# Means and deviations written to memory element by element, the first rows loaded in halves, and two steps of unit 0 moved

## The chip, the cores and the metric

One core of one Trainium2 chip runs the whole program. The metric is the device time of one execution in microseconds (us). Three runs of the kernel before took 761.16, 761.40 and 761.79 us; the median is 761.4.

## The reference, cut to what matters

`x` is the input `u`, 4 sequences of 1024 tokens with 1024 features, seen as 4096 rows. Each row is normalised (mean subtracted, divided by its deviation), and the normalised rows `xn` go through two branches:

```
xn  = (x - mean) / sqrt(var + 1e-5)                # per row, 1024 features
ug  = xn * sigmoid(xn @ gate_w.T + gate_b)         # attention branch
s   = c * G * cumsum(b * ug / G) + d_eff * ug      # d_eff uses the mean of ug over each sequence
h   = silu(silu(xn @ w1.T) @ w3.T) @ w2.T          # 1024 x 1024 weights
ffn = zeros(4096, 1024); ffn[expert index] += gate share * h   # top 2 of 8 experts, used as row numbers
out = x + s * silu(ffn)
```

Since an expert's index is used as a row number, only the first 8 rows of `ffn` are ever filled; silu(0) = 0, so all other rows of the output equal `x`. The three products of all 4096 rows with 1024 x 1024 weights (w1; the gate, for the first sequence alone; w3) are what takes the time.

## The kernel before, in words

**Tiles and units.** The rows are cut into 4 units of 1024. A pass of products is one unit through one weight matrix. There are 9 passes, numbered n: 0 to 3 are w1 on units 0 to 3, 4 (`GATE`) is the gate on unit 0, and 5 to 8 are w3 on the four units. Each pass is a 2 x 2 block product done with 7 block products instead of 8 (`i` from 0 to 6, in chains that share sums), each of 4 output tiles `j` of 128 x 512. A tile takes 4 times 3 TensorE products of 128x128 with 128x512: every operand is split into a high and a low part (names with r, `wh..`, `wl..`, `x..r`), and the helper `three` (lines 1012 to 1015) multiplies high by high, high by low and low by high.

**Order of the work.** One list, made by `plan()` (lines 90 to 311), holds every step in order; each engine walks through the same list and takes the steps of its kind, with semaphores between engines. So a step's place in the list sets what stands ahead of it on its engine. `at(n, i, j, ...)` hangs a step behind the product tile at place `i`, `j` of pass `n` (`i` counts places in the pass; negative ones reach back into the pass before). The steps before the first tile are written out by hand (lines 250 to 259).

**The start.** Unit 0 is loaded as rows of 128 x 1024 (`ROW`, line 726; rows 0 to 7 each with a buffer or a share of two). VectorE takes the statistics (`NA`, lines 1196 to 1198: two `bn_stats` over halves, one aggregate), or ScalarE does (`NS`, through the helper `squares`, lines 867 to 871), POOL raises the variance to the power -0.5 (lines 822 and 823), VectorE normalises (`NB`, line 1209), TensorE turns the rows (`TR`, line 1033), ScalarE copies the turned rows out of PSUM twice, as high part and as full value (`TE`, lines 881 and 883), and VectorE subtracts for the low part (`TL`, through the helper `tt` at line 1159). The first block of w1 comes in four pieces (`W0`, line 729) and is split by ScalarE (`WH0`, line 887) and VectorE (`WO0`). The first block product of unit 0 is done in halves of 256 tokens (`MP`, two halves of four steps `k`, each step 12 products of 256 columns). `WARM` (line 1023) are turnings of an identity that nobody reads, 34 at the start and 12 before the first `MP`. Later in pass 0 the rows 4 to 7 follow tile by tile, and `LQ` (line 1080) multiplies the router's weights with the turned rows of the unit.

**Units 1 to 3.** They come from memory already turned (`XL`, line 751), so their means and deviations are needed along the free dimension, the same on every partition. For each group of four rows of 128 tokens (rows 8 to 31; half a unit, `h`): the rows are loaded as they are (`ROW`), ScalarE sums and squares them (`STAT`, `squares`), save for rows 11 and 15 (`BN_ROWS`), which VectorE does (lines 1203 to 1205). POOL makes `mvu` of them (`MVC`, lines 834 to 845): 128 partitions x 2 (mean, deviation) x 4 rows. `MV` brings them to memory: TensorE turns `mvu` into PSUM (`spare`, lines 1089 to 1097), ScalarE copies the 8 x 128 result to `mvs` (lines 965 to 970), SP writes it to `mv_d` (line 759). `BC` (line 765) loads it back to all 128 partitions, and VectorE subtracts and multiplies the unit's blocks (`LN`, lines 1233 to 1240). There are six such groups; `MVC` is placed 1 or 2 tiles behind the group's last `STAT`, `MV` and `BC` both 4 or 5 tiles behind it.

**Queues.** SP issues nearly all loads in the list's order, and a wait on SP holds all that stands behind it; ScalarE issues the stores of the tiles (`ST`). ScalarE splits operands (`HI`, `WH`, lines 901 and 914) and VectorE makes their low parts (`LO`, `WO`); the sums of weight blocks are `S`.

Of the kernel before, what the change touches and what calls it, by code (L numbers as in the profile page):

```python
# [5 lines left out]
P = 128  # L6
D = 1024
KT = D // P
TOK = 4096
SEQ = 1024  # L10
UT = 1024
HT = 512
E = 8
# [5 lines left out]

BN_ROWS = (11, 15)  # L20
NU = 4
# [10 lines left out]
ACT = mybir.ActivationFunctionType  # L32
# [57 lines left out]
def plan():  # L90
# [3 lines left out]
    def at(n, i, j, *step):  # L94
        g = 7 * n + i
        extra.setdefault((g // 7, g % 7, j), []).append(step)

    for n in range(NN):
        ln = 0 < n < GATE
        if n == 0:  # L100
# [32 lines left out]
            at(0, 4, 0, "RT", 0)  # L133
            at(0, 4, 0, "WO", 0, 5)
            at(0, 4, 1, "RA", 1)
            at(0, 4, 1, "WH", 0, 6)
            at(0, 4, 1, "HI", 0, 6)
# [3 lines left out]
        else:  # L141
# [9 lines left out]
            if ln:  # L151
# [8 lines left out]
                c = 2 * n  # L160
# [25 lines left out]
        if 0 < n < GATE:  # L186
            if n == 1:
                when = [(0, i, j) for i, j in ((2, 1), (2, 3), (3, 0), (3, 1), (3, 3), (4, 0), (4, 2), (4, 3))]
            else:
                when = [(n - 1, i, j) for i, j in ((-1, 0), (-1, 2), (0, 1), (0, 3), (1, 2), (2, 2), (3, 2), (4, 1))]  # L190
            for t, (m, i, j) in enumerate(when):
                r = n * 8 + t
                at(m, i, j, "STAT", r)
                if r < 8 * GATE - 2:
                    at(m, i, j, "ROW", r + 2)
                if t % 4 == 3:
                    k = 4 * i + j
                    c, v = (1, 4) if r == 11 else (2, 5)
                    at(m, *divmod(k + c, 4), "MVC", 2 * n + t // 4)
                    at(m, *divmod(k + v, 4), "MV", 2 * n + t // 4)  # L200
                    at(m, *divmod(k + v, 4), "BC", 2 * n + t // 4)
# [29 lines left out]
        if n >= GATE:  # L231
            for r in range(8):
                s = 8 * (n - GATE) + r
# [8 lines left out]
    for k in range(3):  # L242
# [44 lines left out]
    for k, (n, i, j) in enumerate(tiles):  # L287
# [4 lines left out]
        p = rank(n, i) % 7  # L292
# [68 lines left out]

def program(nc, x, xT, wB, w11, w2T, small, out):
    steps = plan()
# [9 lines left out]
    def nth(kind, *a):  # L373
        return turn[(kind, *a)]
# [3 lines left out]
    for s in steps:  # L378
        if s[0] == "XL":
            q = place[s[1:]]  # L380
# [23 lines left out]
    mv_d = nc.dram_tensor("mv_d", (2 * NU, 2, HT), F32).ap()  # L404

    with ExitStack() as ctx:
        def sb(name, shape, dt=F32):
            return ctx.enter_context(nc.sbuf_tensor(name, shape, dt))
# [4 lines left out]
        def sem(name):  # L413
            return ctx.enter_context(nc.semaphore(name))
# [40 lines left out]
        y = sb("y", [P, KT, E])  # L455
        mvs = sb("mvs", [E, P])

# [36 lines left out]

        s_row = [sem(f"s_row{i}") for i in range(8)]
        s_pl = [sem(f"s_pl{i}") for i in range(PLACES)]
        s_wl = [sem(f"s_wl{i}") for i in range(7)]
# [46 lines left out]
        s_mv = sem("s_mv")  # L544
        s_mvt = sem("s_mvt")
        s_mvs = sem("s_mvs")
        s_mvd = sem("s_mvd")
# [25 lines left out]
        def row_buf(r):  # L573
            if r in (4, 5) or r >= 8:
                return rows[:, r % 2, :]
            p = (6, 6, 5, 5, None, None, 4, 4)[r]
            return w_f(p, 0)[:, 2 * (r % 2):2 * (r % 2) + 2, :].rearrange("p a n -> p (a n)")

        def row_loaded(wait, r):
            if r < 8:  # L580
                wait(s_row[r], 16)
            else:
                wait(s_row[4 + r % 2], 16 * ((r - 8) // 2 + 2))
# [131 lines left out]
        def _(eng):  # L715
            wait = Waiter(eng)
            ncopy = 0
            for s in steps:
                kind = s[0]
                if kind == "ROW":  # L720
# [3 lines left out]
                    elif r >= 8:  # L724
                        wait(s_tr, 2 * (r - 3))
                    eng.dma_start(row_buf(r), x[r * P:(r + 1) * P, :]).then_inc(s_row[r if r < 8 else 4 + r % 2], 16)
                elif kind == "W0":
# [29 lines left out]
                elif kind == "MV":  # L757
                    wait(s_mvs, nth(*s))
                    eng.dma_start(mv_d[s[1]].rearrange("r (t p) -> (r t) p", p=P), mvs[:, :]).then_inc(s_mvd, 16)
                elif kind == "BC":  # L760
# [35 lines left out]
        def _(eng):  # L796
# [20 lines left out]
            for s in steps:  # L817
# [13 lines left out]
                elif kind == "MVC":  # L831
# [4 lines left out]
                    if k > 2:  # L836
                        wait(s_mvt, k - 2)
                    if last in BN_ROWS:
# [19 lines left out]
        def _(eng):  # L858
# [3 lines left out]
            def link(ins):  # L862
                count[0] += 1
                ins.then_inc(s_ac, 1)
                wait(s_ac, count[0])

            def squares(row, total, square, where):
# [5 lines left out]
            for s in steps:  # L873
# [79 lines left out]
                elif kind == "STAT":  # L953
# [10 lines left out]
                    squares(row_buf(r), acs[:, h, 0, t:t + 1], acs[:, h, 1, t:t + 1], row_buf(r)).then_inc(s_st2, 1)  # L964
                elif kind == "MV":
                    k = nth(*s)
                    wait(s_mvt, k)
                    if k > 1:
                        wait(s_mvd, 16 * (k - 1))
                    eng.activation(mvs[:, :], spare[0:E, 0:P], ACT.Copy).then_inc(s_mvs, 1)  # L970
                elif kind == "LE":
# [37 lines left out]
        def _(eng):  # L1009
# [7 lines left out]
            for s in steps:  # L1017
                kind = s[0]
                if kind == "WARM":
                    wait(s_id, 1)  # L1020
                    idle = main[0] if s[1] else spare
                    for q in range(12 if s[1] else 34):
                        eng.transpose(idle[:, q % 4 * P:(q % 4 + 1) * P], ident[:, :], ident[:, :])
# [59 lines left out]
                elif kind == "RA":  # L1083
# [4 lines left out]
                    ins.then_inc(s_ra, 1)  # L1088
                elif kind == "MV":
                    k = nth(*s)  # L1090
                    wait(s_mv, k)
                    if k > 1:
                        wait(s_mvs, k - 1)
                    else:
                        wait(s_ter, 16)
                    eng.matmul(spare[0:E, 0:P], mvu[:, (k - 1) % 2, :, :].rearrange("p r t -> p (r t)"), ident[:, :],
                               start=True, stop=True).then_inc(s_mvt, 1)
                elif kind == "PH":
# [3 lines left out]
                    wait(s_rt, 2 * NU)  # L1102
                    wait(s_mvs, 2 * (NU - 1))
                    u = n - L2
# [43 lines left out]
        def _(eng):  # L1148
# [3 lines left out]
            def link(ins):  # L1152

                count[0] += 1
                ins.then_inc(s_dv, 1)
                wait(s_dv, count[0])
# [32 lines left out]
            for s in steps:  # L1189
                kind = s[0]  # L1190
                if kind == "NA":
                    t = s[1]
                    row_loaded(wait, t)
                    src = row_buf(t)
                    st = bst[:, nth(*s) % 2, :]
                    eng.bn_stats(st[:, 0:6], src[:, 0:HT])
                    link(eng.bn_stats(st[:, 6:12], src[:, HT:D]))
                    eng.bn_aggr(mv0[:, t, :], st).then_inc(s_na, 1)
# [293 lines left out]
```

## Time and profile before

| | |
|---|---|
| median of 3 runs | 761.4 us |
| profiled execution | 761.42 us |
| its span (first to last instruction) | 759.6 us |
| instructions | 8804 |
| granted TensorE clock, mean | 1.000 |
| products with 128x512 or 128x256 columns (lines 1013 to 1015) | 3 x 1024 |

Times in the profile are counted from the start of the span. PE is TensorE's products, PEld its weight loads, DVE is VectorE, ACT ScalarE, POOL GpSimd, SPq the queue of SyncE. A row of the timeline gives its start, its length, engine, line, operation, result and operands (buffer numbers as the allocator gave them), how many like it follow without a break, and in brackets the idle time of the engine just before it and what ended that. Products overlap: what counts for TensorE's pace is the distance from one start to the next, not the length of a row. The rows' names are those of buffers: `wh6f` and `wh5f` hold the first rows of x, `wl2f` the first block of w1, `x0f` to `x8f` the blocks of a unit, `x3r` and `x5r` the low parts at the start.

### The profile page before, as it was taken

To read this page: it belongs to the slowest core of one execution; us is meant where nothing else is said; L and a number is where in the kernel's file an instruction comes from. 1 tells how busy PE (TensorE), PEld (TensorE's weight loads), DVE (VectorE), ACT (ScalarE), POOL (GpSimd) and SP (SyncE) were. 2 spreads that over 40 slices of the span, in tenths; PEclk is the share of its full clock that TensorE was granted. 3 is DMA by queue.
4 is the path that set the end of the run, shared out by engine and by line. 5 is a ranking of instruction groups with operands and counts; after the bars stand their busy time and mean duration, and the time that the engine had idled before them with its cause. 6 is when DMAs were issued, how large, how long until landed. Compare 5 with 4: busy or idle time off the path is not lost.

```text
span 759.6 us, 8804 instructions
## 1 busy us (share of the span) xinstructions
PE 749.9 (99%) x3580; PEld 597.8 (79%) x3580; DVE 508.2 (67%) x477; ACT 343.2 (45%) x441; POOL 41.8 (6%) x56
## 2 busy tenths in 40 slices
PE   8999999999999999999999999999999999999997
PEld 7867877887788787888788878878788778877875
DVE  6889888775958485469999997574525462456321
ACT  5869674845572425232943372225123331324122
POOL 3302103020301000000000000000000000000000
PEclk9999999999999999999999999999999999999999
DMA  9644763547442534466596713241231323110500
GB/s 353 266 167 167 265 228 131 205 143 225 150 156 94 194 112 152 192 209 234 197 360 207 287 56 138 111 153 42 110 139 48 146 84 121 45 56 1 223 1 3
DMA packets 27400, 117.20 MB, mean 154 GB/s; under 512 B 3440, under 2 KB 3680, under 8 KB 20320
## 3 DMA queue, kind: packets, MB, share of 16 engines
q1 hardware_dynamic: 18112, 99.85, 36.5%
q10 hardware_dynamic: 9248, 16.80, 5.9%
q8 instruction: 28, 0.46, 0.3%
q14 instruction: 12, 0.10, 0.0%
HBM read 95.60 MB, written 37.77 MB: 176 GB/s over the span
## 4 chain that ended last, share of the span: by engine, by line
PE 82%; DVE 10%; issue 4%; ACT 3%; DMA 0%; POOL 0%; DVEq 0%
PE main L1013 26%; PE main L1015 26%; PE main L1014 26%; PE lgp L1080 1%; PE spare L1107 1%; PE lgp L1107 1%; DVE x3r L1159 1%; DVE x2f L1159 1%; DVE wl3f L1159 1%; DVE x1f L1159 1%; DVE wl5f L1159 1%; DVE x8f L1159 0%; PE main L1142 0%; DMA wh6f<-x 0%; DVE s L1159 0%
## 5 line engine op out<-in xcount | busy, mean ns | idle before, releaser
L1159 DVE TENSOR_TENSOR s<-s,main 128x512 f32<-128x512 f32 x72 | 48.5, 683 | 60.1 <-PE main L1015 60.1
L1159 DVE TENSOR_TENSOR u<-u,main 128x512 f32<-128x512 f32 x36 | 24.4, 685 | 41.8 <-PE main L1015 41.8
L922 ACT ACTIVATE s<-main 128x512 f32<-128x512 f32 x36 | 20.8, 596 | 55.1 <-PE main L1015 23.4
L941 ACT ACTIVATE u<-u 128x512 f32<-128x512 f32 x32 | 20.2, 632 | 54.5 <-DVE u L1159 54.4
L1159 DVE TENSOR_TENSOR u<-s,main 128x512 f32<-128x512 f32 x32 | 21.7, 685 | 32.5 <-PE main L1015 32.5
L941 ACT ACTIVATE rows<-rows 128x512 f32<-128x512 f32 x16 | 10.1, 632 | 71.3 <-DVE rows L1159 71.3
L941 ACT ACTIVATE s<-s 128x512 f32<-128x512 f32 x32 | 20.0, 630 | 47.8 <-DVE s L1159 47.8
L1159 DVE TENSOR_TENSOR rows<-s,main 128x512 f32<-128x512 f32 x16 | 11.0, 688 | 30.4 <-PE main L1015 30.4
L941 ACT ACTIVATE u<-main 128x512 f32<-128x512 f32 x32 | 18.7, 592 | 20.5 <-PE main L1015 20.5
L871 ACT ACTIVATE rows<-rows,nm 128x1024 f32<-128x1024 f32 x22 | 25.4, 1154 | 0.7
L869 ACT ACTIVATE rows<-rows 128x1024 f32<-128x1024 f32 x23 | 24.2, 1050 | 0.1
L1013 PE MATMUL main<-x2r,wh0r 128*128 128x256 f32 (+1 forms) x48 | 15.7, 326 | 1.1 <-DVE x3r L1159 0.8
L855 POOL MEMSET tail<- 128x1024 f32 x1 | 1.0, 955 | 269.9 <-PE main L1015 269.9
L1015 PE MATMUL main<-x2r,wl0r 128*128 128x256 f32 (+1 forms) x48 | 15.2, 318 | 0.0
L1159 DVE TENSOR_TENSOR x6r<-x6f,x4r 128x2048 fp32r<-128x2048 f32 x3 | 6.9, 2289 | 8.8 <-ACT x4r L901 8.8
L1013 PE MATMUL main<-x6r,wh3r 128*128 128x512 f32 x32 | 12.5, 392 | 0.0
L1014 PE MATMUL main<-x6r,wh0r 128*128 128x512 f32 x32 | 12.5, 390 | 0.0
L1015 PE MATMUL main<-x6r,wl3r 128*128 128x512 f32 x32 | 12.5, 389 | 0.0
L1014 PE MATMUL main<-x5r,wh1r 128*128 128x512 f32 x32 | 12.5, 389 | 0.0
L1014 PE MATMUL main<-x5r,wh2r 128*128 128x512 f32 x32 | 12.5, 389 | 0.0
L1014 PE MATMUL main<-x4r,wh4r 128*128 128x512 f32 x32 | 12.4, 389 | 0.0
L1014 PE MATMUL main<-x8r,wh3r 128*128 128x512 f32 x32 | 12.4, 389 | 0.0
(703 smaller groups left out, 2427.1 us busy)
## 6 DMA issues: line engine op xcount, KB each, us to landing
out<-x SPq DMA_DIRECT2D x31, 512.0 KB, 7.9
rows<-x SPq DMA_DIRECT2D x26, 512.0 KB, 4.3
H_d<-u ACTq DMA_DIRECT2D x32, 256.0 KB, 3.9
H_d<-s ACTq DMA_DIRECT2D x16, 256.0 KB, 3.7
rows<-xh_d SPq DMA_DIRECT2D x16, 256.0 KB, 5.2
w2f<-w2T SPq DMA_DIRECT2D x2, 2048.0 KB, 9.8
wl6f<-wB SPq DMA_DIRECT2D x3, 1024.0 KB, 8.2
wl4f<-wB SPq DMA_DIRECT2D x3, 1024.0 KB, 6.0
```

The lines of the kernel that those rows point to most:

```text
L855: eng.memset(tb[:, 0:D], 0.0).then_inc(s_oz, 1)
L869: link(eng.activation(row, row, ACT.Copy, accum_out=total))
L871: return eng.activation(where, row, ACT.Square, bias=nm[:, 0:1], accum_out=square)
L922: eng.activation(s1[:, j, :], bk, ACT.Copy).then_inc(s_pa, 1)
L941: ins = eng.activation(dst, src, ACT.Silu)
L1013: eng.matmul(o, sh, mh, start=first, stop=False, skip_group_check=True)
L1014: eng.matmul(o, sh, ml, start=False, stop=False, skip_group_check=True)
L1015: return eng.matmul(o, sl_, mh, start=False, stop=last, skip_group_check=True)
L1080: ins = eng.matmul(lgp[h][Q * q:Q * (q + 1), :], wr32[:, NQ * kh + q, :], xf(n, b)[:, q, :], start=(kh == 0), stop=(kh == 1))
L1107: ins = eng.matmul(acc[o][Q * j:Q * (j + 1), :], Pz[:, 8 * u + 4 * h + j, :], c_buf(n, i, j), start=(u == 0 and h == 0), stop=(u == NU - 1 ...
L1159: return eng.tensor_tensor(o, a, b, op)
```

## The change

- **Means to memory.** `MV` becomes one transfer of SP alone, straight from `mvu` to `mv_d`: 128 partitions x 2 x 4 single elements of 4 bytes. TensorE's turning, ScalarE's copy, `mvs` and their semaphores go. `MV` waits for POOL's `MVC`, and is placed `c + 2` tiles behind the last `STAT`, one tile earlier than before and one ahead of `BC`. POOL waits for the transfer before it writes a buffer of `mvu` again.
- **Rows 0 and 1 in halves.** Each is loaded by two transfers of 128 x 512 from a new input `x01` that holds these halves one after the other; the first `bn_stats` waits for the first half alone.
- **Order at the start.** `NA` of row 2 goes behind the low parts of rows 0 and 1, `WO0` of step 1 ahead of them; `WO0` of step 2 and `NA` of row 3 follow. `WARM` has 29 and 14 turnings for 34 and 12.
- **A Silu first.** ScalarE does one Silu on a column before its other steps; its result is written over later.
- **Unit 0's pieces.** Row 15's statistics go from VectorE to ScalarE and two places later (from place 4, tile 3 to place 5, tile 1), with the load of row 17; `WH` of block 6 goes one tile earlier (from place 4, tile 1 to tile 0).

```diff
-BN_ROWS = (11, 15)
+BN_ROWS = (11,)
...
+            at(0, 4, 0, "WH", 0, 6)
             at(0, 4, 1, "RA", 1)
-            at(0, 4, 1, "WH", 0, 6)
...
-                when = [(0, i, j) for i, j in ((2, 1), (2, 3), (3, 0), (3, 1), (3, 3), (4, 0), (4, 2), (4, 3))]
+                when = [(0, i, j) for i, j in ((2, 1), (2, 3), (3, 0), (3, 1), (3, 3), (4, 0), (4, 2), (5, 1))]
...
-                    c, v = (1, 4) if r == 11 else (2, 5)
+                    c, v = (1, 4) if r in (11, 15) else (2, 5)
                     at(m, *divmod(k + c, 4), "MVC", 2 * n + t // 4)
-                    at(m, *divmod(k + v, 4), "MV", 2 * n + t // 4)
+                    at(m, *divmod(k + c + 2, 4), "MV", 2 * n + t // 4)
                     at(m, *divmod(k + v, 4), "BC", 2 * n + t // 4)
...
-             ("WH0", 0), ("WH0", 1), ("TE", 0, 0), ("TE", 1, 0), ("WO0", 0), ("NA", 2), ("TL", 0, 0), ("TL", 1, 0), ("MP", 0, 0),
-             ("WH0", 2), ("WO0", 1), ("MP", 0, 1), ("WH0", 3), ("TE", 0, 1), ("TE", 1, 1), ("NA", 3), ("NB", 2),
-             ("WO0", 2), ("MP", 0, 2), ("NB", 3), ("TR", 2), ("TR", 3), ("WO0", 3), ("MP", 0, 3), ("WH", 0, 1),
+             ("WH0", 0), ("WH0", 1), ("TE", 0, 0), ("WO0", 0), ("TE", 1, 0), ("WO0", 1), ("TL", 0, 0), ("TL", 1, 0), ("MP", 0, 0), ("MP", 0, 1),
+             ("NA", 2), ("WH0", 2), ("WO0", 2), ("MP", 0, 2), ("NA", 3), ("WH0", 3), ("TE", 0, 1), ("TE", 1, 1),
+             ("NB", 2), ("TR", 2), ("WO0", 3), ("NB", 3), ("TR", 3), ("MP", 0, 3), ("WH", 0, 1),
...
+                    c0 = 0
+                    if r < 2:
+                        c0 = HT
+                        eng.dma_start(row_buf(r)[:, 0:HT], x01[r, 0]).then_inc(s_rh[r], 16)
+                    src = x01[r, 1] if r < 2 else x[r * P:(r + 1) * P, :]
+                    eng.dma_start(row_buf(r)[:, c0:D], src).then_inc(s_row[r if r < 8 else 4 + r % 2], 16)
...
                 elif kind == "MV":
-                    wait(s_mvs, nth(*s))
-                    eng.dma_start(mv_d[s[1]].rearrange("r (t p) -> (r t) p", p=P), mvs[:, :]).then_inc(s_mvd, 16)
+                    k = nth(*s)
+                    wait(s_mv, k)
+                    if k > 1:
+                        wait(s_mvd, 16 * (k - 1))
+                    eng.dma_start(mv_d[s[1]].rearrange("r (t p) -> p r t", p=P), mvu[:, s[1] % 2, :, :],
+                                  allow_slow_non_contiguous=True).then_inc(s_mvd, 16)
...
+            wait(s_po, 3)
+            eng.activation(nm[:, :], mhalf[:, 0:1], ACT.Silu)
...
-                elif kind == "MV":
-                    k = nth(*s)
-                    wait(s_mvt, k)
-                    if k > 1:
-                        wait(s_mvd, 16 * (k - 1))
-                    eng.activation(mvs[:, :], spare[0:E, 0:P], ACT.Copy).then_inc(s_mvs, 1)
...
-                    for q in range(12 if s[1] else 34):
+                    for q in range(14 if s[1] else 29):
...
-                    eng.matmul(spare[0:E, 0:P], mvu[:, (k - 1) % 2, :, :].rearrange("p r t -> p (r t)"), ident[:, :],
-                               start=True, stop=True).then_inc(s_mvt, 1)
...
+                    if t < 2:
+                        wait(s_rh[t], 16)
+                    else:
+                        row_loaded(wait, t)
                     eng.bn_stats(st[:, 0:6], src[:, 0:HT])
+                    row_loaded(wait, t)
                     link(eng.bn_stats(st[:, 6:12], src[:, HT:D]))
```

## Rows read from the trace of the kernel before

**Rows 1.** The page, first lines: span, then busy time (share) and instructions of each engine.

```profile
span 759.6 us, 8804 instructions
...
PE 749.9 (99%) x3580; PEld 597.8 (79%) x3580; DVE 508.2 (67%) x477; ACT 343.2 (45%) x441; POOL 41.8 (6%) x56
```

**Rows 2.** Waits of PE: line, what it waited for, us in total, times, longest.

```profile
PE main L1013 <- DVE x3r L1159: 1.1, 2, 0.8
...
PE main L1013 <- DVE x6r L1159: 0.4, 1, 0.4
```

**Rows 3.** Timeline of the first 21 us, several engines.

```profile
4.10 0.69 DVE L1196 BATCH_NORM_STATS2 bst<-wh6f 128x6 f32<-128x512 f32 x1 [4.10 <-DMA wh6f<-x]
...
6.99 1.27 ACT L887 ACTIVATE wh0r<-wl2f 128x512 fp32r<-128x512 f32 x2 [4.97 <-DMA wl2f<-w]
...
9.91 0.69 DVE L1196 BATCH_NORM_STATS2 bst<-wh5f 128x6 f32<-128x512 f32 x1
...
10.64 0.59 ACT L883 ACTIVATE x0f<-lgp 128x512 f32<-128x512 f32 x1
...
11.35 1.24 DVE L1159 TENSOR_TENSOR x3r<-x0f,x2r 128x512 fp32r<-128x512 f32 x2
...
12.65 0.39 PE L1013 MATMUL main<-x2r,wh0r 128*128 128x256 f32 x1 [0.79 <-DVE x3r L1159]
...
16.38 0.81 DVE L1209 TENSOR_SCALAR wh5f<-wh5f,mv 128x1024 f32<-128x1024 f32 x1 [0.46 <-POOL mv L823]
...
17.50 0.60 PE L1033 MATMUL main<-ident,wh5f 128*128 128x128 f32 x4
...
20.98 0.39 PE L1013 MATMUL main<-x2r,wh0r 128*128 128x256 f32 x1
```

**Rows 4.** Timeline around 40 us, ScalarE and PE.

```profile
36.95 1.28 ACT L941 ACT_TABLE_LOAD   x1
...
42.82 1.06 PE L1080 MATMUL lgp<-x0f,cst 128*32 128x512 f32 x8 [1.26 <-ACT x7f L883]
```

**Rows 5.** PE's timeline around one turning, then the group of all of them.

```profile
171.75 0.39 PE L1014 MATMUL main<-x2r,wh5r 128*128 128x512 f32 x1
171.97 0.39 PE L1015 MATMUL main<-x0r,wl5r 128*128 128x512 f32 x1
172.29 0.38 PE L1096 MATMUL spare<-ident,mvu 128*8 128x128 f32 x2
...
172.94 0.39 PE L1014 MATMUL main<-x2r,wh5r 128*128 128x512 f32 x1
...
L1096 PE MATMUL spare<-ident,mvu x12: 272/274/276, 75.1 to 254.8; 128*8 128x128 f32 x12
```

**Rows 6.** Waits of SP's queue: us in total, times, longest.

```profile
SPq L759 <- ACT mvs L970: 25.5, 6, 9.4
```

**Rows 7.** Timeline of SP's queue, 75 to 86 us.

```profile
76.14 0.43 SPq L751 DMA_DIRECT2D x4f<-xT  x1
...
84.14 0.35 SPq L759 DMA_DIRECT2D mv_d<-mvs  x1
...
85.37 0.34 SPq L765 DMA_DIRECT2D bc<-mv_d  x1
```

**Rows 8.** Landings: of the broadcast (KB, median us); of the w2 loads (shortest, median, longest).

```profile
bc<-mv_d SPq DMA_DIRECT2D x6, 512.0 KB, 3.8
...
DMA to landing us min/median/max: 7.5/9.8/12.1
```

**Rows 9.** Timeline of VectorE, 82 to 92 us.

```profile
82.19 2.29 DVE L1159 TENSOR_TENSOR wl6r<-wl6f,wh6r 128x2048 fp32r<-128x2048 f32 x1 [1.91 <-ACT wh6r L914]
...
87.20 0.69 DVE L1203 BATCH_NORM_STATS2 bst<-rows 128x6 f32<-128x512 f32 x1
...
91.19 4.61 DVE L1159 TENSOR_TENSOR x2f<-x2f,bc 128x2048 f32<-128x2048 f32 x2
```

**Rows 10.** The chain of waits: start, us, what; one 256-column product.

```profile
16.47 0.12 PE main L1015
```

More of the change, by code:

```diff
@@ L359, in places_of, with program @@
     raise ValueError("no place for the last rows")
-def program(nc, x, xT, wB, w11, w2T, small, out):
+def program(nc, x, x01, xT, wB, w11, w2T, small, out):
     steps = plan()
@@ L455, in program @@
         y = sb("y", [P, KT, E])
-        mvs = sb("mvs", [E, P])
         def w_f(p, part):
@@ L495, in program @@
         s_row = [sem(f"s_row{i}") for i in range(8)]
+        s_rh = [sem(f"s_rh{i}") for i in range(2)]
         s_pl = [sem(f"s_pl{i}") for i in range(PLACES)]
@@ L544, in program @@
         s_mv = sem("s_mv")
-        s_mvt = sem("s_mvt")
-        s_mvs = sem("s_mvs")
         s_mvd = sem("s_mvd")
@@ L725, in _ @@
                         wait(s_tr, 2 * (r - 3))
-                    eng.dma_start(row_buf(r), x[r * P:(r + 1) * P, :]).then_inc(s_row[r if r < 8 else 4 + r % 2], 16)
+                    c0 = 0
[4 more added lines that the diff above has]
+                    eng.dma_start(row_buf(r)[:, c0:D], src).then_inc(s_row[r if r < 8 else 4 + r % 2], 16)
                 elif kind == "W0":
@@ L836, in _ @@
                     if k > 2:
-                        wait(s_mvt, k - 2)
+                        wait(s_mvd, 16 * (k - 2))
                     if last in BN_ROWS:
@@ L1088, in _ @@
                     ins.then_inc(s_ra, 1)
[L1089 to L1095, printed above, removed]
-                    eng.matmul(spare[0:E, 0:P], mvu[:, (k - 1) % 2, :, :].rearrange("p r t -> p (r t)"), ident[:, :],
-                               start=True, stop=True).then_inc(s_mvt, 1)
                 elif kind == "PH":
@@ L1102, in _ @@
                     wait(s_rt, 2 * NU)
-                    wait(s_mvs, 2 * (NU - 1))
                     u = n - L2
@@ L1192, in _ @@
                     t = s[1]
-                    row_loaded(wait, t)
                     src = row_buf(t)
                     st = bst[:, nth(*s) % 2, :]
+                    if t < 2:
+                        wait(s_rh[t], 16)
+                    else:
+                        row_loaded(wait, t)
                     eng.bn_stats(st[:, 0:6], src[:, 0:HT])
+                    row_loaded(wait, t)
                     link(eng.bn_stats(st[:, 6:12], src[:, HT:D]))
@@ L1480 @@
         "x": np.ascontiguousarray(t["L0_attn_u"].reshape(TOK, D)),
+        "x01": np.ascontiguousarray(t["L0_attn_u"].reshape(TOK, D)[:2 * P].reshape(2, P, 2, HT).transpose(0, 2, 1, 3)),
         "xT": np.ascontiguousarray(t["L0_attn_u"].reshape(NU, 2, HT, 2, 4, P).transpose(0, 3, 1, 5, 4, 2)),
```

## The prediction

> **What bounds the kernel now.** I read the page first: TensorE is busy for 99% of the span, VectorE for 67%, ScalarE for 45% [rows 1]. A busy PE is a modelled figure here, so I went on to the waits of PE and to the timelines, to find where its instructions start later than the ones before them allow. Away from a few places one 128x512 product starts 0.22 to 0.23 us after the other, all the way to the end. The time is therefore the sum of what PE has to do, plus its start, plus those few places, and an edit pays only if it takes work or a hole from PE. The reader should see four of them.
>
> First, the start. PE begins the first product at 12.65 and the fifth step of products at 20.98, both times held by VectorE's x3r [rows 2, 3]. Second, a hole of 1.26 us before the logits at 42.82, ended by a ScalarE copy (x7f); ScalarE loaded a table for 1.28 us just ahead of that copy, at 36.95 [rows 4]. Third, 0.4 us at the first product of unit 1, again ended by VectorE (x6r) [rows 2]. Fourth, the turning itself: from 171.97 to 172.94 two products and the turning start, 0.97 us where two starts at 0.22 to 0.23 would be 0.45. So one turning costs PE 0.52 us, far more than its two passes, because the products on either side of it are spaced wider too; twelve records are two for each of six [rows 5].
>
> The profiled execution took 761.42 us, its span 759.6; the median of the three runs shown is 761.4, so a sum made against the profile needs no correction.
>
> **The change, part by part.**
>
> *The turning goes.* Six times 0.52 us leave PE, 3.1 us in all, and PE has no other work to wait for there. ScalarE loses the six copies behind them, SP's wait for those copies (25.5 us in six times [rows 6]) becomes a wait for POOL, which is done before ScalarE's copy. What comes in is a transfer of 2x4 single elements from each of 128 partitions, 1024 pieces, where eight pieces of 512 bytes went. No row shows a transfer of single elements. Below: the present one lands at most 1.23 us after its issue, since the broadcast that waits for it is issued at 85.37 against 84.14 [rows 7]. Above: the two w2 loads, 512 pieces of 4 KB each, landed after 7.5 and 12.1 us [rows 8]; they are the same number of pieces with a thousand times the bytes. A gain on today's 1.23 is excluded, since nothing in it is taken away. I take 3 us, nearer the lower row, because the pieces carry four bytes.
>
> What does that cost? Nothing as long as the broadcast is in time. The tightest case is the first one. SP stands at that point right behind the x4f load, issued at 76.14 [rows 7], which will be about 74 with the 2.1 us that the start and the table load bring (below). The broadcast lands 3.8 us after its issue [rows 8], with 0.3 for issuing. Its user is the subtraction at 91.19 [rows 9]. VectorE will come to it 2.1 us earlier for the same reason, up to 1.9 for a wait that goes and 1.4 for statistics that go, so at 85.8; but the adds ahead of it wait for PE's tiles, which come 2.1 + 0.5 earlier, so 88.6 at the latest. I take 87. That leaves 87 - 74 - 4.1, some 9 us for the transfer, three times what I take. If it needs more, LN is late first, then the products of unit 1. Behind SP's wait stand row loads and the next x blocks; as long as the transfer stays under those 9 us SP is freed earlier than today.
>
> The Trainium skill (DMA: Bandwidth & Descriptors, Rules for kernel authors) speaks against this edit: a strided last dimension makes one descriptor per element, and one should arrange it otherwise; for a transposition by rearranged access it names a 19-fold difference. That would be an estimate of 19 x 1.23, some 23 us, and the sum would lose all its gain; no run so far shows it.
>
> *The start.* Rows 0 and 1 come as two halves. The first statistics begin when all of row 0 has landed, at 4.10 [rows 3]. With halves the first one (0.69 us) can lie beside the second half's transfer. It gains between nothing, or a little less with two more issues on SP, and 0.69; I take 0.5, since its second half may still have to be awaited a little. That carries to the turned rows. Next, the statistics of row 2 stand at 9.91 and hold VectorE for 1.44 us, until the two x3r at 11.35 [rows 3]. Moved behind them, x3r waits instead for ScalarE's copy that starts at 10.64 and takes 0.59, so 11.23, with the 0.5 about 10.7. The second x3r then ends about 11.4 and PE starts at 11.5 in place of 12.65. The warm-up turnings (29 for 34, 14 for 12) only fill PE's waits on either side.
>
> Not all of that lasts. VectorE now does row 2's and row 3's statistics later, and row 3's normalisation, at 16.38 behind POOL [rows 3], comes at about 16.7. But PE could turn rows 2 and 3 only at 17.50, behind the third step of products, though row 3 was ready at 17.19. Now the third step is done at 11.5 + 36 x 0.12 = 15.8 (one 256-column product takes 0.12 in the chain [rows 10]), row 2 is turned at once and row 3 at 17.5 to 17.6, where it had stood behind row 2's eight turnings, at some 18.4 by estimate. From there the old distance to 20.98 gives 20.1: 0.9 us gained. The ends are 0.3 (the halves bring nothing and VectorE's row 3 keeps its 0.3 us of delay) and 1.4 (PE never waits again from 11.4 on: 48 products of 0.12 and sixteen turnings at 0.60 for four [rows 3] end at 19.6).
>
> *The table load.* A Silu on ScalarE ahead of all else puts its table there at the start, where ScalarE waits 4.97 us for weights anyway [rows 3]. The 1.28 us at 36.95 go. The copies of the last two rows come that much earlier, and the hole at 42.82 closes but for some 0.1: 1.2 us from PE. That only holds if copies and squares do not call the old table back; after 36.95 they run with Silu and no third load appears in the trace. The Trainium skill (ScalarE: Activation LUTs, What ACT_TABLE_LOAD costs) gives a switch some 2.66 us with its drain; the trace has 1.28 and the next instruction right behind it, so I take 1.28, and the hole is the limit either way.
>
> *Two pieces of unit 0.* Row 15's statistics go from VectorE (1.44 us as at 9.91, here from 87.20) to ScalarE, which is busy for less than half of the span and has room there; the split of wh6 is issued one tile earlier, so VectorE's 1.91 us wait at 82.19 goes [rows 9]. VectorE then reaches unit 1's blocks before PE does, and the 0.4 us at its first product [rows 2] go. If that cover fails, the 0.4 us stay and up to another 0.5 joins them.
>
> **The sum.** 0.9 + 1.2 + 0.4 + 3.1 = 5.6 us, and 761.42 - 5.6 = 755.8.
>
> **The rivals.**
>
> *Halves bring nothing.* The transfers may follow one another no faster, and the two extra issues push the weights back. For it: ScalarE waits at 6.99 for the first weights [rows 3], so DMA sets the pace there too. Against it: the statistics order alone shortens the wait for x3r. Then the start gives 0.3 or nothing, and the time is 756.4 to 756.7.
>
> *The single elements come late (slower than before).* This is one mechanism: if an engine's 64 elements are not streamed but each waits for its write, at a quarter of 1.23 us apiece, a transfer takes 64 x 0.31 + 1.2 = 21 us. The first broadcast is then 12 us beyond its 9, PE waits for unit 1, and the time is 755.8 + 12, about 768. It decides from 9 us on, and from 9 + 5.6 + 1.5 = 16 us (0.23 us an element) the kernel is slower than before. For it speaks that no row shows such pieces; against it, that 512 pieces landed in 7.5 us with 4 KB each. The skill's warning named above is this rival, with its own figure of 23 us and some 770.
>
> *The table load stays.* If the compiler loads a table for the copies again, the 1.2 us stay: 757.0. The single load in the trace behind the first Silu speaks against it.
>
> **How the numbers follow.** Forecast as summed: 0.64, with its own range 754.6 to 757. Halves bring nothing: 0.15. Late elements: 0.14, of which 0.03 stay below 759.9, 0.03 come out within 0.2% of now and 0.08 above. Table load stays: 0.05. The rest, 0.02, is something that I don't see, most likely near no change. Below, the start at its far end (1.4) and the whole 1.3 us hole give 755.2, and waits too small for the view may close with them, so 754.4; above, a forecast without start and table load gives 757.9, and a transfer of 12 us, 3 beyond its 9, gives 758.8. So 754.4 to 759.2. A measurement of this kernel tells 0.2%, or 1.5 us, from no change: faster by more 0.64 + 0.15 + 0.05 + 0.03 = 0.87, within it 0.03 + 0.02 = 0.05, slower 0.08.
>
> **What would show it.** Right: no PE record of the turning, products at 0.23 us through those places; first product near 11.5, the fifth step near 20.1; one table load, at the start; the logits of unit 0 near 40.7 with a wait of a tenth; broadcast issued within 5 us of the element transfer. Wrong: SP waiting over 9 us at the broadcast, VectorE's first subtraction in unit 1 released by a DMA, a second table load near 35, or the first statistics still at 4 us.

## The result, and the profile after

The change takes 766.4 us, median of 6 runs (765.3 to 767.9), beside 761.4 for the kernel before on the same chip: 1.0068 of its time, 95% interval 1.0058 to 1.0079. It is slower by 5 us, where 755.8, a gain, was forecast, and it lies outside the range of 754.4 to 759.2. The profiled execution took 766.27 us.

The first lines of the page of the changed kernel, to be held against [rows 1]:

```profile
span 764.2 us, 8759 instructions
...
PE 749.1 (98%) x3565; PEld 598.1 (78%) x3565; DVE 507.0 (66%) x474; ACT 342.1 (45%) x440; POOL 39.8 (5%) x54
```

TensorE's busy time fell by less than 1 us, while the span grew by 4.6: it stands still more than before. Two steps of the chain of waits of the changed kernel, from 74 to 101 us (start, us, what), say where:

```profile
74.93 14.67 DMA mv_d<-mvu
...
89.62 6.45 DMA bc<-mv_d
```

VectorE's timeline behind it:

```profile
96.17 4.62 DVE L1154 TENSOR_TENSOR x2f<-x2f,bc 128x2048 f32<-128x2048 f32 x2 [8.34 <-DMA bc<-mv_d]
```

The first transfer of single elements, issued behind the load of x4f (1024 KB), lands after 14.67 us. The broadcast that waits for it needs 6.45 more, and VectorE's subtraction starts at 96.17 instead of 91.19 [rows 9], after 8.34 us without work. That a DMA releases it is a sign that the prediction named for being wrong; so is a wait of SP of over 9 us at the broadcast, at most 11.1 here. The queue of SP and the landings of the transfer (line 765) in the changed kernel show how the row load beside it fared:

```profile
74.46 0.43 SPq L754 DMA_DIRECT2D x4f<-xT  x1
74.93 0.43 SPq L765 DMA_DIRECT2D mv_d<-mvu  x1
78.44 0.34 SPq L729 DMA_DIRECT2D rows<-x  x1
89.62 0.33 SPq L772 DMA_DIRECT2D bc<-mv_d  x1
...
DMA to landing us min/median/max: 10.6/11.7/14.7
```

All six transfers are slow, 10.6 us at best. The row load issued at 78.44 landed 12.9 us later, where the same load took 4.5 before; ScalarE stood 5.67 us for it. Broadcasts land after 6.3 us in the median, 3.8 before [rows 8]. All DMA of the core is slow in that stretch. From 80 to 89.5 us, in the changed kernel and then in the kernel before (the last two columns are the busy share of the DMA engines and the GB/s that they moved):

```profile
80.00:89.50 9.50, 9.50 (x44) 7.86 (x43) 6.28 (x8) 5.44 (x10) 0.00 (x0) 1.00 0.77 34
```

```profile
80.00:89.50 9.50, 9.50 (x43) 7.86 (x43) 7.56 (x10) 7.83 (x12) 0.52 (x3) 1.00 0.63 219
```

The engines count as busy, but they move 34 GB/s instead of 219.

What it costs TensorE stands in its waits and its timeline around 100 us:

```profile
PE main L1018 <- DVE u L1154: 4.1, 2, 3.5
```

```profile
97.59 0.39 PE L1020 MATMUL main<-x5r,wl6r 128*128 128x512 f32 x1
101.44 0.79 PE L1018 MATMUL main<-x5r,wh6r 128*128 128x512 f32 x1 [3.46 <-DVE u L1154]
102.03 0.63 PE L1019 MATMUL main<-x7r,wh6r 128*128 128x512 f32 x1
102.46 0.63 PE L1020 MATMUL main<-x5r,wl6r 128*128 128x512 f32 x1
...
106.30 0.63 PE L1020 MATMUL main<-x5r,wl6r 128*128 128x512 f32 x1
108.76 0.50 PE L1018 MATMUL main<-x1r,wh0r 128*128 128x512 f32 x1 [1.84 <-DVE x6r L1154]
```

The wait at 101.44 is not for the late data. It is for the add `u`, with which VectorE takes a finished tile out of PSUM and which stands behind the late subtraction in VectorE's order. After the wait the products start 0.43 us apart instead of 0.23. The stretch before the wait and the one behind it have the granted clock in the column after POOL's busy time:

```profile
92.00:97.60 5.60, 5.60 (x27) 4.62 (x25) 1.43 (x1) 2.98 (x7) 1.47 (x3) 1.00 1.06 363
101.40:106.50 5.10, 5.06 (x12) 3.80 (x12) 5.07 (x4) 4.92 (x7) 0.00 (x0) 0.50 0.53 60
```

The granted clock was 0.50, that is 1.2 GHz, for the twelve products from 101.44 on. At 108.76 TensorE waits again, for x6r, which VectorE makes after the subtractions.

**The account.** What TensorE's starts lost from 97 us on, beyond its pace before: 3.6 at 101.44; 2.6 in the slow products (0.36 + 11 x 0.20); 2.2 at 108.76; 0.84 at 166.59 and 0.69 at 221.08: 9.9 us. Against it stand 1.7 that start and table load gave (the first product with `wh4` comes at 67.30, before at 68.99), 3.1 for the turnings and 0.5 for the old hole in unit 1: 9.9 - 5.3 = 4.6, the growth of the span.

The other edits did what they say. The Silu's table load stands at the start of ScalarE, and the logits of unit 0 begin without a wait (compare [rows 4]); two rows of the changed kernel's timeline:

```profile
0.74 1.28 ACT L876 ACT_TABLE_LOAD   x1 [0.74 <-PEq L1466]
...
41.17 1.06 PE L1085 MATMUL lgp<-x0f,cst 128*32 128x512 f32 x8
```

The start gained less than forecast. Its timeline in the changed kernel, to be read against [rows 3]:

```profile
3.64 0.70 DVE L1194 BATCH_NORM_STATS2 bst<-wh6f 128x6 f32<-128x512 f32 x1 [3.64 <-DMA wh6f<-x]
...
6.38 0.69 DVE L1196 BATCH_NORM_STATS2 bst<-wh6f 128x6 f32<-128x512 f32 x1 [0.32 <-DMA wh6f<-x]
...
12.20 0.38 PE L1018 MATMUL main<-x2r,wh0r 128*128 128x256 f32 x1
...
17.32 0.81 DVE L1208 TENSOR_SCALAR wh5f<-wh5f,mv 128x1024 f32<-128x1024 f32 x1 [0.46 <-POOL mv L830]
...
18.19 0.66 PE L1038 MATMUL lgp<-ident,wh5f 128*128 128x128 f32 x4 [0.55 <-DVE wh5f L1208]
...
20.75 0.39 PE L1018 MATMUL main<-x2r,wh0r 128*128 128x256 f32 x1
```

The first half of row 0 is there 0.46 us earlier, but the second half of row 1 has to be awaited until 6.38. The first product comes 0.45 us earlier; row 3 is normalised 0.94 later than before, and at the fifth step 0.23 us are left.

### The profile page after: what moved, and what is told of

Same layout as the page of the kernel before. It is cut to its first block, busy times and chain, and to the rows that moved or that the text cites. A ratio compares the mean times of both kernels' runs of the same rounds, so it can differ in the third digit from the quotient of the medians.

```text
span 764.2 us, 8759 instructions
## 1 busy us (share of the span) xinstructions
PE 749.1 (98%) x3565; PEld 598.1 (78%) x3565; DVE 507.0 (66%) x474; ACT 342.1 (45%) x440; POOL 39.8 (5%) x54
## 4 chain that ended last, share of the span: by engine, by line
PE 74%; DVE 10%; DMA 7%; issue 4%; ACT 4%; POOL 0%; SPq 0%; ACTq 0%; DVEq 0%
PE main L1018 23%; PE main L1020 23%; PE main L1019 23%; DMA mv_d<-mvu 2%; DMA bc<-mv_d 2%; DMA H_d<-x6f 2%; DMA x7f<-xT 1%; DVE x1f L1154 1%; PE spare L1102 1%; PE lgp L1102 1%; PE lgp L1085 1%; DVE x8f L1154 1%; DVE x6f L1154 1%; DVE x5r L1154 1%; DVE x2f L1154 1%
## 5 line engine op out<-in xcount | busy, mean ns | idle before, releaser
L850 POOL TENSOR_SCALAR mvu<-acs 128x4 f32<-128x4 f32 (+1 forms) x6 | 7.3, 1216 | 158.0 <-ACT rows L882 157.9
L952 ACT ACTIVATE x6f<-x6f 128x512 f32<-128x512 f32 x8 | 4.9, 624 | 17.0 <-DVE x6f L1154 17.0
```

The lines of the kernel that those rows point to most:

```text
L850: eng.tensor_scalar(mvu[:, h, 0, 0:m], acs[:, h, 0, 0:m], 1.0 / D, None, ALU.mult)
L952: ins = eng.activation(dst, src, ACT.Silu)
```

## The experiments

Times are medians beside the kernel before on the same chip. It took 761.3 to 761.5 us in every batch, so runs of different batches are compared as they are.

**1. The change without its new transfer.** TensorE's turning, ScalarE's copy and the transfer of eight pieces are kept, all else is as in the change.

```diff
-                    eng.dma_start(mv_d[s[1]].rearrange("r (t p) -> p r t", p=P), mvu[:, s[1] % 2, :, :],
-                                  allow_slow_non_contiguous=True).then_inc(s_mvd, 16)
+                    eng.dma_start(mv_d[s[1]].rearrange("r (t p) -> (r t) p", p=P), mvs[:, :]).then_inc(s_mvd, 16)
```

> The change with TensorE's turning kept for the means (TensorE, ScalarE copy, eight runs of 512 bytes); all else as in the change. Theory (the single elements land too slowly, all else of the change is good): no late broadcast, no long wait of PE, so before less the table load (1.3), the start (0.2 as seen) and unit 0's hole (0.4): 759.3 us, between 758.8 and 760.0. Rival (the moved pieces of unit 0, row 15 on ScalarE above all, make VectorE or PE wait): the wait of PE near 97 us stays and the time is 762 or more.

759.83 us, 0.9982 of before (0.9972 to 0.9991). TensorE begins unit 1 without a wait, at a granted clock of 1.00 from 90 to 110 us; in this kernel:

```profile
101.69 0.50 PE L1023 MATMUL main<-x1r,wh0r 128*128 128x512 f32 x1
```

So the loss is the transfer's, and the other edits together gain 1.5 us (761.33 before in this batch).

**2. The new transfer alone**, in the kernel before (the reverse edit).

> The kernel before with the transfer of single elements alone. Theory: the transfer lands 10 us or more after its issue, VectorE waits some 8 us for the first broadcast and PE for some 4 to 6 us in unit 0's last block, less 3.1 us of turnings: 763 to 769 us. Rival (the order is at fault, not the transfer): the turnings leave, nothing else happens, 758.3 us.

765.82 us, 1.0056 (1.0041 to 1.0071). The same landings and much the same loss without any of the other edits, but what is late first is another transfer: VectorE, which here still takes row 15's statistics, stands 4.06 us for that row and then only 0.84 us for the broadcast. The landings of line 759, and VectorE's wait, in this kernel:

```profile
DMA to landing us min/median/max: 10.3/11.6/14.7
```

```profile
91.13 0.69 DVE L1188 BATCH_NORM_STATS2 bst<-rows 128x6 f32<-128x512 f32 x1 [4.06 <-DMA rows<-x]
```

**3. 256 pieces of 16 bytes.** Four neighbouring tokens go to each partition (the rows are loaded in another order), so a partition's four values are one run in memory.

```diff
                     src = x01[r, 1] if r < 2 else x[r * P:(r + 1) * P, :]
+                    if r >= 8:
+                        g = r // 4
+                        src = x[4 * g * P:4 * (g + 1) * P, :].rearrange("(p t) n -> t p n", t=4)[r % 4]
-                    eng.dma_start(mv_d[s[1]].rearrange("r (t p) -> p r t", p=P), mvu[:, s[1] % 2, :, :],
+                    eng.dma_start(mv_d[s[1]].rearrange("r (p t) -> p r t", t=4), mvu[:, s[1] % 2, :, :],
```

> The change, but each statistics load takes rows 4p+t to partition p, so that a partition's four means lie side by side and go as runs of 16 bytes: 256 pieces instead of 1024; nothing else is moved. Theory (landing time goes with the number of pieces, about 10 us for 1024): it lands in 3.5 to 4.5 us, no broadcast is late, 756.0 to 757.0 us. Rival (the order or SP's place is at fault): PE's long wait stays, over 762 us. Rival (the landing goes with the partitions or with writing to memory at all): it lands in 8 to 12 us as now, over 760 us.

758.55 us (757.47 to 760.77), 0.9967 (0.9958 to 0.9977): a gain, but 1.5 us above the upper end expected. The profiled execution is the slowest of the ten, so its waits may be longer than those of the others. The landings of line 768, and the waits of VectorE and TensorE, in this kernel:

```profile
DMA to landing us min/median/max: 3.5/5.0/8.0
```

```profile
90.89 4.62 DVE L1157 TENSOR_TENSOR x2f<-x2f,bc 128x2048 f32<-128x2048 f32 x2 [2.48 <-DMA bc<-mv_d]
...
103.49 0.50 PE L1021 MATMUL main<-x1r,wh0r 128*128 128x512 f32 x1 [2.20 <-DVE x6r L1157]
```

The slowest is again the first, 8.0 us. It was issued at 77.29, half a microsecond behind the load of x4f on the same queue; its broadcast left at 85.27 and took 5.5 us, so VectorE stood for it.

**4. 512 pieces of 8 bytes.** Only the write differs from the change: two neighbouring values of a partition go side by side. The row loads are not reordered with it, so the means reach other tokens than their own; the kernel serves for its time alone.

> The change with the same bytes moved as 512 pieces of 8 bytes; the means and deviations arrive in another order of tokens. Theory (landing goes with the number of pieces): 6 to 7 us from issue to landing, under the 9 us that I had found free, so hardly a wait of PE: 756 to 758 us. Rival (not the pieces): 11 to 12 us as now and 764 us or more.

759.69 us in its one run, 1.7 above what was expected, with landings of 3.9, 5.9 and 9.3 us (shortest, median, longest). Twice the pieces of run 3 land less than 1 us later in the median (5.9 against 5.0), and twice these again, in the change, 6 later. So the landing doesn't go with the number of pieces; what single elements have beside their number was left to runs 11 and 12. A wait of TensorE of 2.66 us, by the starts, was left at the head of unit 1.

**5. Pieces of 16 bytes, the first transfer one step earlier**, ahead of the load of x4f, and its broadcast one step earlier.

```diff
+                    early = r == 11
-                    at(m, *divmod(k + c + 2, 4), "MV", 2 * n + t // 4)
-                    at(m, *divmod(k + v, 4), "BC", 2 * n + t // 4)
+                    at(m, *divmod(k + c + 2 - early, 4), "MV", 2 * n + t // 4)
+                    at(m, *divmod(k + v - early, 4), "BC", 2 * n + t // 4)
```

> The element-free form with 16-byte pieces (256 of them), and for the first group only the transfer is issued one step earlier, ahead of the load of x4f, and the broadcast one step earlier too. Theory (the landing is the queue ahead plus the pieces): the first transfer is issued at about 73.5 us instead of 77.3, lands in 3.5 to 4.5 us instead of 8.0, bc is in SBUF by 85, VectorE's wait of 2.48 us for bc at 90.9 and TensorE's of 2.36 us at 101 to 103.5 go, and the seven products at half clock behind it run at full clock: 754.8 to 755.8 us. Rival (a transfer of many pieces delays what is queued with it, whenever it is issued, so the load of x4f or the broadcast is late instead): TensorE still stands still for over 1.5 us between 90 and 104 us, 757.5 to 758.8 us.

756.39 us, 0.9938 (0.9924 to 0.9953); the kernel is 0.6 us above the upper end expected, but all the waits named are gone. SP's queue, the first landing (line 769), and VectorE's subtraction in this kernel:

```profile
73.15 0.38 SPq L769 DMA_DIRECT2D mv_d<-mvu  x1
...
76.09 0.43 SPq L758 DMA_DIRECT2D x4f<-xT  x1
76.56 0.43 SPq L776 DMA_DIRECT2D bc<-mv_d  x1
...
DMA to landing us min/median/max: 2.2/2.2/2.2
```

```profile
87.98 4.61 DVE L1158 TENSOR_TENSOR x2f<-x2f,bc 128x2048 f32<-128x2048 f32 x2
```

Ahead of the megabyte the same transfer lands in 2.2 us instead of 8.0. VectorE comes to the subtraction at 87.98 and waits for nothing; the prediction had it there at 87.

**6. Single elements, the first transfer one step earlier**: the edit of run 5 in the change itself.

> The change as it is, with 1024 single elements, but the first group's transfer and broadcast one step earlier, the transfer ahead of the load of x4f. Theory (the pieces themselves take the time): the first transfer, issued at about 73 us, still needs 10 us or more, the broadcast is issued at 83 to 84.5 us and lands by 88 to 91, so the waits of 3.5 us of TensorE and the half clock behind them mostly go: 757 to 760 us; transfers queued while the pieces drain are late. Rival (the queue ahead made most of the 14.7 us): it lands in 6 to 7 us, no wait is left, 755.5 to 756.5 us. Second rival (early or late, the pieces hold other transfers up so that row 15 becomes the late one): 763 us or more.

767.65 us, 1.0082 (1.0067 to 1.0097): worse than the change, the last of the three ways expected. Rows of SP's queue, then of VectorE and ScalarE, in this kernel:

```profile
73.95 0.39 SPq L766 DMA_DIRECT2D mv_d<-mvu  x1
...
84.96 0.33 SPq L773 DMA_DIRECT2D bc<-mv_d  x1
```

```profile
92.64 4.62 DVE L1155 TENSOR_TENSOR x2f<-x2f,bc 128x2048 f32<-128x2048 f32 x2 [3.80 <-DMA bc<-mv_d]
...
86.80 1.06 ACT L881 ACTIVATE rows<-rows 128x1024 f32<-128x1024 f32 x1 [4.51 <-DMA rows<-x]
```

With nothing of a megabyte ahead of it the transfer still holds the broadcast back for 11.0 us, so these are the pieces' own; the queue ahead made the other 4 of the 14.7. Now the load of x4f is behind the elements, and loads of x4f land after 11.3 us in the median (6.4 in run 5). The rows are late for ScalarE too. An earlier place did not mend a transfer that holds up its neighbours.

**7. Rows 0 and 1 whole**, and the start in the order of before, in the kernel of run 1.

> The change with TensorE's turning kept (the kernel of the first run) and, in addition, rows 0 and 1 loaded whole, in the order of the start of the kernel before. If the halves bring what the traces show at the fifth step (20.79 us with them, 20.79 to 20.98 without), this runs at 759.8 to 760.2 us, within 0.3 us of the kernel with halves (759.83). If they bring the 0.9 us of the prediction, 760.6 to 760.9 us.

759.44 us, 0.9974 (0.9965 to 0.9984), which the intervals can't tell from run 1's 759.83. The fifth step begins at 21.02 here, 20.79 there. The halves and the new order of the start bring nothing that the time shows.

**8. Without the first Silu**, in the kernel of run 1.

```diff
-            wait(s_po, 3)
-            eng.activation(nm[:, :], mhalf[:, 0:1], ACT.Silu)
```

> The change with TensorE's turning kept and without the early Silu on ScalarE. If the table load stood on the path as predicted, it is back at about 37 us, the wait of TensorE at about 42 us of 1.2 us is back, and the time is 760.9 to 761.2 us (1.2 more than 759.83). Rival (the first load at the start is only moved, and a later wait takes up the gain): within 0.3 us of 759.83.

760.89 us, 0.9993 (0.9983 to 1.0003): 1.06 more than run 1. The table load is back at 37.09, and so is the wait, in TensorE's timeline of this kernel:

```profile
42.95 1.07 PE L1088 MATMUL lgp<-x0f,cst 128*32 128x512 f32 x8 [1.33 <-ACT x7f L891]
```

**9. Row 15's sums and W(0,6) in their old places**, in the kernel of run 1.

> The change with TensorE's turning kept, and with the two pieces of unit 0's work back in their old places (row 15's sums on VectorE, the rounding of W(0,6) one step later). If they are worth what the prediction gave them, the wait of 0.4 us of TensorE in unit 1 is back: 760.1 to 760.4 us against 759.83. Rival (the wait was hidden by what comes behind it): within 0.2 us of 759.83.

760.23 us, 0.9986 (0.9976 to 0.9996): 0.4 more than run 1, no more than the 0.39 by which run 7 was faster, so the times alone can't tell them apart. What tells them apart is the wait in TensorE's timeline, 0.36 us here and none in run 1 at the same product:

```profile
102.32 0.50 PE L1023 MATMUL main<-x1r,wh0r 128*128 128x512 f32 x1 [0.36 <-DVE x6r L1169]
```

**10. Run 5 with rows 0 and 1 whole** and the start of before.

> 16-byte pieces, the first transfer one step earlier, rows 0 and 1 whole in the old order of the start; the table load and the two pieces of unit 0 as in the change. If the halves cost a little, as the last comparison has it (759.44 without against 759.83 with), 755.9 to 756.2 us. Rival (the halves bring the 0.23 us that the first trace showed): 756.5 to 756.8 us.

756.18 us, 0.9931 (0.9916 to 0.9946; 756.11 to 756.26): 5.25 us faster than before, the fastest here, and again no worse without the halves. The gap to run 7, which differs in the way of the means to memory alone (with the order of the row loads and the earlier first broadcast that go with it), is 3.26 us. Product by product, TensorE's lead over run 7 grows in steps of 0.41 to 0.49 us at the six turnings, 2.6 in all; smaller steps between them make the rest.

**11. The transfer by itself.** Seven extra transfers that nothing reads, one after the other, in the kernel of run 10, between 660 and 700 us:

```diff
+                    eng.dma_start(pr_d[2, 0:1024].rearrange("(q p t) -> p q t", p=P, t=2), one.rearrange("p (q t) -> p q t", t=2),
+                                  allow_slow_non_contiguous=True).then_inc(s_pr, 16)
+                    wait(s_pr, 48)
+                    eng.dma_start(pr_d[3, 0:512].rearrange("(q p) -> p q", p=P), one[:, 0:4],
+                                  allow_slow_non_contiguous=True).then_inc(s_pr, 16)
+                    wait(s_pr, 64)
...
```

> The kernel of the run before with seven extra transfers from mvu to memory that nothing reads, in the stretch from 660 to 700 us in which no other transfer of SyncE is queued, each issued when the one before has landed: 256 pieces of 16 bytes twice, 512 of 8, 512 of 4, 1024 of 4, 1024 of 8, 256 of 4. Theory A (the size of 4 bytes is what is slow): 512 of 4 bytes take 5 us or more, 1024 of 8 bytes under 7 us, 1024 of 4 bytes 10 to 11 us. Theory B (the number of pieces in one transfer is what is slow, past 512): 512 of 4 bytes land in about 4 us as 512 of 8 do, and 1024 of 8 bytes take 10 to 11 us as 1024 of 4 do. Under either 256 pieces land in 2 to 3.5 us. The kernel's own time stays that of the run before unless the seven together pass 698 us.

SP's queue in this kernel; each issue waits for the landing before, so the distance to the next row is the landing (16 bytes twice, then 512 x 8, 512 x 4, 1024 x 4, 1024 x 8, 256 x 4 bytes):

```profile
660.43 0.43 SPq L792 DMA_DIRECT2D pr_d<-mvu  x1
665.22 0.37 SPq L795 DMA_DIRECT2D pr_d<-mvu  x1
666.86 0.36 SPq L798 DMA_DIRECT2D pr_d<-mvu  x1
670.60 0.36 SPq L801 DMA_DIRECT2D pr_d<-mvu  x1
680.17 0.36 SPq L804 DMA_DIRECT2D pr_d<-mvu  x1
690.23 0.36 SPq L807 DMA_DIRECT2D pr_d<-mvu  x1
694.42 0.36 SPq L810 DMA_DIRECT2D pr_d<-mvu  x1
```

The first transfer stood behind a load of x8f, issued at 660.07, and took 4.8 us; the same 256 pieces of 16 bytes with nothing ahead took 1.6, 512 of 8 bytes 3.7, 1024 of 8 bytes 4.2. But 512 of 4 bytes took 9.6, 1024 of 4 bytes 10.0, and 256 of 4 bytes still 7.8. It is not the number; by this run it is the 4 bytes. The kernel itself took 756.16 us in its one run.

The time does not go into sending the pieces. For the 512 of 4 bytes, issued at 670.60, two stretches of this kernel (the last two columns are the busy share of the DMA engines and GB/s):

```profile
671.40:671.90 0.50, 0.50 (x4) 0.38 (x4) 0.00 (x0) 0.38 (x1) 0.00 (x0) 1.00 0.50 4
671.90:680.10 8.20, 8.20 (x38) 6.80 (x37) 3.76 (x2) 3.60 (x4) 0.00 (x0) 1.00 0.00 0
```

All their packets lie in the first half microsecond; then the engines carry nothing for 8.2 us until the landing is reported.

**12. 4 bytes, side by side or 64 bytes apart**, in the same place.

```diff
+                    eng.dma_start(pr_d[1, 0:512].rearrange("(q p) -> p q", p=P), one[:, 0:4],
+                                  allow_slow_non_contiguous=True).then_inc(s_pr, 16)
+                    eng.dma_start(pr_d[2, :].rearrange("(q p u) -> p q u", p=P, u=16)[:, :, 0:1],
+                                  one[:, 0:4].rearrange("p (q t) -> p q t", t=1), allow_slow_non_contiguous=True).then_inc(s_pr, 16)
```

> The kernel of the probe with other extra transfers in the same stretch, each issued when the one before has landed: 256 pieces of 16 bytes (behind the load of x8f), 512 of 4 bytes to adjacent addresses, 512 of 4 bytes to addresses 64 bytes apart, 512 of 8 bytes 64 bytes apart, 128 of 4 bytes adjacent, 256 of 16 bytes. Theory (the size of a piece alone decides): 512 of 4 bytes take 9 to 10 us at either spacing, and 128 of 4 bytes over 5 us. Rival (4-byte pieces are slow where neighbouring pieces, sent by different partitions, go into the same 64 bytes): 512 of 4 bytes 64 bytes apart take 3 to 5 us like 512 of 8 bytes. 256 of 16 bytes take 1.6 us again.

SP's queue in this kernel, in the order of the expectation, from the second on:

```profile
664.98 0.37 SPq L794 DMA_DIRECT2D pr_d<-mvu  x1
673.08 0.36 SPq L797 DMA_DIRECT2D pr_d<-mvu  x1
676.39 0.36 SPq L800 DMA_DIRECT2D pr_d<-mvu  x1
678.43 0.33 SPq L803 DMA_DIRECT2D pr_d<-mvu  x1
685.25 0.36 SPq L806 DMA_DIRECT2D pr_d<-mvu  x1
```

The theory that the size alone decides falls. 512 single elements to adjacent addresses took 8.1 us, the same 512 set 64 bytes apart 3.3; 512 of 8 bytes 64 bytes apart took 2.0, and only 128 adjacent single elements still 6.8. What is slow is a single element of 4 bytes written next to others; 8 bytes to adjacent addresses were not (3.7 in run 11). In every slow case the neighbour came from another partition; whether that matters was not varied. Each number is one landing, and repeated forms differ by up to 1.6 us (16 bytes with nothing ahead: 1.6 and 3.2; 512 adjacent single elements: 9.6 and 8.1), which doesn't touch 3.3 against 8.1. Why such neighbours are slow, and whether spacings between 4 and 64 bytes are, stays open.

## Why the prediction was wrong

**The step that failed** is the landing of the single elements: "I take 3 us, nearer the lower row, because the pieces carry four bytes." It is 11.7 in the median and 14.7 where it matters. Two things were missed. The size counted the wrong way: pieces of 16 bytes land in 1.6 us and pieces of 8 in 3.7, adjacent single elements in 7.8 to 10.0 (run 11). And the lower row, 1.23 us, was read from a transfer that went out with nothing fresh ahead of it; the new one stands right behind the load of x4f, which the prediction itself noted, and that adds some 4 to 6 us (14.7 against 11.0 in run 6, 8.0 against 2.2 in runs 3 and 5). The upper row was no bound either: its loads are 512 pieces each, half of the new transfer's 1024, and 14.7 lies above their 12.1.

**The limit of 9 us** was derived well on VectorE's side: it is at the subtraction at 87.98 in run 5, forecast 87. But it took the broadcast's 3.8 us as given. In runs 3 and 4 the broadcast took 5.5 and 6.3 us, and landings of 8.0 and 9.3 already made VectorE stand for 2.48 and 2.77.

**The rival "single elements come late"** named what was late, with its break-even at 16 us. Its mechanism, each element waiting for its write in turn, does not fit: 256, 512 and 1024 elements took 7.8, 9.6 and 10.0 us, and the packets are sent within half a microsecond (run 11). By its line 14.7 us, 5.7 beyond the 9, would give 761.5; the change took 766.4. Three costs came on top that the line didn't hold: the broadcast itself landed in 6.45 instead of 3.8 us, TensorE ran twelve products at half clock after its wait (2.6 us), and there were two later stops. The one of 0.84 stands behind a late load of x7f, which SP could issue only after its wait for the third transfer; the one of 0.69 is for a copy of ScalarE, and what it has to do with the landings is not shown.

**The Trainium skill** (DMA: Bandwidth & Descriptors, Rules for kernel authors) spoke against the edit, and by that it was the better guide: one descriptor per element was slow here, by 10.6 against at most 1.23 us, a factor of 8.6 at least where the estimate had 19. Its remedy, a contiguous last dimension, is what run 3 does with four values, and with run 5's place 256 pieces of 16 bytes gave the whole gain. But its reason is not the whole of it here: 512 single elements set 64 bytes apart, single packets as well, landed in 3.3 us (run 12).

**The turnings**: forecast 3.1 us; runs 7 and 10 differ by 3.26. Right, and 2.6 of it stand as steps at the six turnings. The price was read from the spacing of starts, not from the turning's own rows.

**The table load**: forecast 1.2; run 8 shows 1.06 and the 1.33 us wait back. Right, and no second load was called for.

**The two pieces of unit 0**: forecast 0.4; in run 9 the wait of 0.36 is back. Right by the trace; the 0.40 between the times is within what they vary by.

**The start**: forecast 0.9; the trace shows 0.23 at the fifth step, and the time none (runs 7 and 10 against 1 and 5). The rival "halves bring nothing" was right on this part. Here the step that failed is "with the 0.5 about 10.7": row 1's second half had to be awaited until 6.38, so the two x3r are done 0.7 us later than forecast, and the first product came at 12.20 instead of 11.5. Then row 2's statistics, moved behind the low parts, came at 12.06 instead of 9.91, and row 3's normalisation at 17.32 instead of the 16.7 forecast, so TensorE waits for row 3 at 18.19.

With the transfer mended, the sum without the start's 0.9 would be 4.7 us, 756.7; run 10 took 756.18. So the other three terms of the sum held.

## What to carry to other kernels

Give each partition a run of neighbouring values before writing statistics to memory: here pieces of 16 bytes landed in 1.6 to 3.2 us with nothing ahead (2.8 to 6.5 among the other loads of run 10), adjacent single elements in 6.8 to 10.0 (10.6 to 14.7 in the change), and the order of the rows could be chosen at load time at no cost that the time shows. Bound a small transfer's landing together with the large one issued just ahead of it on its queue, and put the small one first; that helped the pieces of 16 bytes (run 5) and not the single elements (run 6). When a wait is to be priced, add what the waiting engine has queued behind it, what other transfers lose meanwhile, and products at half clock, which followed some of TensorE's waits here.

## What was not expected of the hardware

- Single elements of 4 bytes were slow side by side, not for their size alone: 8.1 us for 512 of them adjacent, 3.3 with 64 bytes between their starts.
- Until such a transfer has landed, others land late too, on both queues: a row load took 12.9 us, 4.5 before, and ScalarE's stores of x6f took 11.4 us in the median, 3.8 before. The pieces themselves were sent long since.
- The granted clock fell to 0.50 (1.2 GHz) after TensorE's wait of 3.6 us, by the starts. After a wait of 2.36 us in run 3 it was 0.61 in the mean of the next 3 us, part of them at 1.2 GHz; after 2.66 us in run 4 it stayed at 1.00 (2.4 GHz). The length of the one wait did not decide it in these runs.
